# DeepFM + CIN on one core: four fields looked up by matrix products in place of three, their keys fetched by transfers, the weights' set-up rearranged, and the last tile's rows awaited alone

## What is computed

```python
emb = embed_table[f_ix, x_idx]                        # 2048 x 26 x 16
lin1 = w1_table[f_ix, x_idx].sum(axis=1, keepdims=True) + w1_bias
s = emb.sum(axis=1)
fm = 0.5 * ((s * s).sum(-1) - (emb * emb).sum(axis=(1, 2)))[:, None]
h = relu(emb.reshape(n, F * D) @ mlp_w1 + mlp_b1)     # 416 -> 400
h = relu(h @ mlp_w2 + mlp_b2)                         # 400 -> 400
deepfm = lin1 + fm + h @ mlp_w3 + mlp_b3
x0 = emb.transpose(0, 2, 1); last = x0; feats = []
for W in (cin_w0, cin_w1, cin_w2):                    # 128 x 26 x 26, then 128 x 128 x 26 twice
    last = einsum('ndl,ndf,klf->ndk', last, x0, W)
    feats.append(last)
return deepfm + concatenate(feats, -1).sum(1) @ lin_w + lin_b
```

## Time and profile before

| | before |
|---|---|
| median of 3 runs | 530.3 us (530.12 to 530.62) |
| the profiled execution: time | 530.45 us |
| the profiled execution: span of the core | 528.6 us |
| mean granted TensorE clock | 0.968 |
| TensorE matmuls busy | 468.6 us, 89% |
| VectorE busy | 376.7 us, 71% |
| ScalarE busy | 361.6 us, 68% |
| GpSimd busy | 364.6 us, 69% |

### The profile page before, as it was taken

One profiled execution on the slowest core, in us unless ns is written; L12 is line 12 of the kernel. 1 busy time (PEld: TensorE's weight loads), 2 busy tenths in 40 slices (PEclk: granted clock), 3 DMA queues, 4 the chain that ended last, 5 costly groups with the idle time before them and its releaser, 6 DMA issues. The chain is left out here.

```text
span 528.6 us, 6627 instructions
## 1 busy us (share of the span) xinstructions
PE 468.6 (89%) x2230; PEld 384.6 (73%) x2230; DVE 376.7 (71%) x610; ACT 361.6 (68%) x707; POOL 364.6 (69%) x382
## 2 busy tenths in 40 slices
PE   0798499899898989899999989898989899998895
PEld 0795367588787878687877878787868687787684
DVE  6811265869687786868686968778686868695766
ACT  1002459878686877777676868786777767677883
POOL 5777787877777777777777777777777777774000
PEclk9999559899999999999999999999999999999998
DMA  8973652122222222222222222222222222221000
GB/s 179 237 133 26 82 132 8 5 8 7 9 7 9 7 8 7 9 7 9 7 8 7 8 8 8 8 8 8 8 8 8 8 8 7 8 8 6 0 2 1
DMA packets 21550, 13.63 MB, mean 26 GB/s; under 512 B 12792, under 2 KB 20493, under 8 KB 21261
## 3 DMA queue, kind: packets, MB, share of 16 engines
q0 software_dynamic: 12064, 3.31, 18.4%
q1 hardware_dynamic: 5863, 7.92, 6.4%
q10 hardware_dynamic: 3590, 1.99, 2.0%
HBM read 13.00 MB, written 0.19 MB: 25 GB/s over the span
## 5 line engine op out<-in xcount | busy, mean ns | idle before, releaser
L417 POOL DMA_INDIRECT emb<-rows,idx_raw x377 | 364.3, 966 | 117.4 <-issue 114.6
L660 DVE TENSOR_TENSOR z_lo<-ps_s,z_hi 128x512 fp32r<-128x512 f32 (+1 forms) x192 | 130.7, 687 | 66.5 <-ACT ps_s L483 65.1
L476 ACT ACTIVATE z_hi<-ps_s 128x512 fp32r<-128x512 f32 (+1 forms) x192 | 114.4, 596 | 78.7 <-PE ps_s L908 77.8
L483 ACT ACTIVATE ps_s<-ps_s 128x512 f32<-128x512 f32 (+1 forms) x192 | 113.9, 593 | 0.7
L922 PE MATMUL ps_q<-z_lo,zw_hi 128*127 128x512 f32 (+1 forms) x192 | 86.0, 448 | 15.9 <-DVE z_lo L660 14.4
L923 PE MATMUL ps_q<-z_hi,zw_lo 128*127 128x512 f32 (+1 forms) x192 | 76.4, 398 | 0.0
L924 PE MATMUL ps_q<-z_hi,zw_hi 128*127 128x512 f32 (+1 forms) x192 | 76.3, 397 | 0.0
L908 PE MATMUL ps_s<-xt,pick 128*128 128x512 f32 (+1 forms) x192 | 74.3, 402 | 0.4 <-DVE xt L652 0.4
L922 PEld LDWEIGHTS ps_q<-z_lo,zw_hi 128*127 128x127 f32 (+1 forms) x192 | 36.4, 190 | 32.4 <-DVE z_lo L660 19.7
L994 PE MATMUL ps_y<-look_hi,one_hot 128*128 128x442 f32 (+1 forms) x156 | 56.3, 361 | 2.3 <-DVE one_hot L754 2.3
L995 PE MATMUL ps_y<-look_lo,one_hot 128*128 128x442 f32 (+1 forms) x156 | 54.8, 353 | 0.0
(11 more groups left out here) (165 smaller groups left out, 757.2 us busy)
## 6 DMA issues: line engine op xcount, KB each, us to landing
emb<-rows,idx_raw POOLq DMA_INDIRECT x377, 3.0
w_space<-rows SPq DMA_DIRECT2D x2, 728.9 KB
m_raw<-mlp_w SPq DMA_DIRECT2D x2, 650.0 KB
w<-cin_w SPq DMA_DIRECT2D x1, 832.0 KB, 6.7
w<-cin_w ACTq DMA_DIRECT2D x1, 832.0 KB, 13.2
w_space<-cin_w SPq DMA_DIRECT2D x1, 832.0 KB, 15.0
w_space<-cin_w ACTq DMA_DIRECT2D x1, 832.0 KB, 18.4
m_raw<-rows SPq DMA_DIRECT2D x1, 728.9 KB
```

Of the source, the lines that this page charges most:

```text
L417: pool.indirect_dma_start(emb[t % EMB][:, f, :], None, rows, bass.IndirectOffsetOnAxis(row_ix[:, t, f:f + 1], 0)).then_inc(gathered[t], 16)
L476: act.activation(z_hi[0:k, c, :], ps[0:k, :], ACT.Square)
L483: act.activation(ps[0:k, :], ps[0:k, :], ACT.Square).then_inc(hi_ready, 1)
L660: dve.tensor_tensor(z_lo[0:k, u % NC, :], ps_s[s_no(t, u) % RING][0:k, :], z_hi[0:k, u % NC, :].bitcast(F32), ALU.subtract).then_inc(lo_re ...
```

## The change

- LOOKS is 4: from tile 3 on, 22 fields are gathered and 4 looked up. The split of the tables, KEYS, ROWS and PICKED get new steps; the one-hot is now made in the step that KEYS names; the last `pick_row` stands in `start_tile` ahead of the first `z_low`.
- Keys: TensorE's `keys` is gone. Once, all keys are transposed, copied and stored to DRAM; then SyncE fetches each tile's four rows of keys to all partitions (`key_row`), two buffers.
- Set-up: `cin_w2` comes in two halves of its rows k, and `cin_w1` is issued when the first half has landed; TensorE does 52 half-size products. The blocks of pairs are stored by six transfers (`leave`) and brought back by six (`move`). `m2_raw` shares space with `w2` and is loaded and split during tile 0.
- The second MLP layer's rows are cut 128, 128, 128 and 16; the last chunk holds high and low parts stacked, 10 products in place of 12.
- `x_high` makes only the fp32r copy; the plain copy `x_full` follows the first `square` and is waited for by the second and third `picked`.
- The last tile: its first 18 gathers have their own semaphore; ScalarE copies by position in three parts after the last `square` of tile 14, and TensorE does `hidden2` and `sum_products` of tile 14 ahead of `x_half`; VectorE's `start_last` does all of tile 14 first.

The diff, cut to its core:

```diff
-LOOKS = 3
+LOOKS = 4
+EARLY = 18
-        LOOK_SPLIT = {4: 0, 6: 1, 8: 2}
-        KEYS = {1: 0, 5: 1, 9: 2}
-        ROWS = {3: 0, 7: 1, 11: 2}
-        PICKED = {5: 0, 9: 1}
+        LOOK_SPLIT = {3: 0, 5: 1, 7: 2, 9: 3}
+        KEYS = {4: 0, 7: 1, 9: 2, 11: 3}
+        ROWS = {3: 0, 6: 1, 8: 2, 11: 3}
+        PICKED = {6: 0, 9: 1, 11: 2}
...
+        def move(eng, n):
+            name, g, c0, col, ab, n_b, n_c, n_d = BLOCKS[n]
+            n_a = GROUPS[g]
+            eng.wait_ge(y_stored[n], 16)
+            eng.dma_start(moved[0:n_a * n_c, g, col:col + n_b * n_d].rearrange("p (b d) -> p b d", d=n_d),
+                          bass.AP(y_dram[n].tensor, y_dram[n].offset,
+                                  [[n_d, n_a * n_c], [n_a * n_c * n_d, n_b], [1, n_d]])).then_inc(moved_in[g], 16)
...
-            sp.dma_start(w2[0:HALF_P], cin_w2[0:HALF_P]).then_inc(w2_in, 16)
+            for h in range(2):
+                ls = slice(HALF_P * h, HALF_P * (h + 1))
+                sp.dma_start(w2[0:HALF_P, ls], cin_w2[0:HALF_P, ls]).then_inc(w2_in[h], 16)
+            sp.wait_ge(w2_in[0], 16 * 2)
...
+            for t in range(FIRST_LOOK, T):
+                if t >= FIRST_LOOK + 2:
+                    sp.wait_ge(one_hot_ready, look_no(t - 2, LOOKS))
+                sp.dma_start(key_row[t % 2], key_dram[LOOKS * t:LOOKS * (t + 1), :].partition_broadcast(P)
+                             ).then_inc(keys_in[t % 2], 16)
...
             def x_high(t, h):
-                act.activation(x32[t % 2][LO * h:LO * h + XR], ps, ACT.Copy)
+            def x_full(t, h):
+                act.wait_ge(lo_ready, x_no(t, h) + 1)
+                act.activation(x32[t % 2][LO * h:LO * h + XR], ...
...
+            x_full(0, 0)
+            x_full(0, 1)
             act.wait_ge(m1_in, 16 * 3)
             act.activation(m1_hi[0:XK], m1_raw[0:XK], ACT.Copy).then_inc(m1_hi_ready, 1)
...
                     if looks(t + LEAD):
                         if u in PICKED:
                             pick_row(t + LEAD, PICKED[u])
-                        if u - 2 in KEYS:
-                            keys_to_one_hot(t + LEAD, KEYS[u - 2])
+                        if u in KEYS:
+                            keys_to_one_hot(t + LEAD, KEYS[u])
...
                 add_third(t - 1)
+                if looks(t - 1 + LEAD):
+                    pick_row(t - 1 + LEAD, LOOKS - 1)
                 z_low(t, 0)
                 add_product(t - 1, NQ - 1)
                 z_low(t, 1)
                 fold(t - 1)
                 hidden2(t - 1)
-                if looks(t - 1 + LEAD):
-                    pick_row(t - 1 + LEAD, 2)
                 z_low(t, 2)
...
             def look_rows(t, i):
+                if n:
+                    pe.wait_ge(looked, n)
                 pe.wait_ge(one_hot_ready, n + 1)
...
+                    if after == T - 1:
+                        hidden2(t)
+                        sum_products(t)
+                        x_half(after, 0)
+                        x_half(after, 1)
```

More of the change, by code:

```diff
@@ L515, in start_tile @@
                 x_high(t, 1)
-                for u in range(NC):
-                    square(t, u)
+                square(t, 0)
+                x_full(t, 0)
+                x_full(t, 1)
+                square(t, 1)
+                square(t, 2)
             act.wait_ge(b_done, 1)
@@ L728, in tile, with start_last @@
                             pick_row(t + LEAD, PICKED[u])
-                        if u - 2 in KEYS:
-                            keys_to_one_hot(t + LEAD, KEYS[u - 2])
+                        if u in KEYS:
+                            keys_to_one_hot(t + LEAD, KEYS[u])
+            def start_last():
+                t = T - 1
+                times_left(t - 1, NQ - 1)
+                times_third(t - 1)
+                add_third(t - 1)
+                add_product(t - 1, NQ - 1)
+                fold(t - 1)
+                hidden2(t - 1)
+                x_low(t, 0)
+                x_low(t, 1)
+                for u in range(NC):
+                    z_low(t, u)
             def start_tile(t):
```

276 lines of the change are left out of this document (172 added, 104 removed).

## The result

The changed kernel takes **559.4 us** (median of 4 runs, 558.0 to 560.3) against 530.2 (530.0 to 530.6) for the one before, measured beside it: 1.055 times as long, interval 1.052 to 1.057. My prediction was 543.3, with a range of 508 to 551. The sign and the places were right, the size wasn't: +12.9 us were forecast, +29 came. The profiled execution of the change took 558.02 us, with a span of 556.2; the one before had 528.6.

The account below looks back on a forecast made before the run. Bound: the 77.1 us set-up, then TensorE's order of work with small waits. Set-up -11.6, tile 0 +3.1, 13 look-up tiles +20.2, end +1.2: +12.9 on 530.45, so 543.3 us; range 508 to 551, the forecast's own 532 to 551.

Parts of the forecast that it names:

- Set-up, forecast -11.6: Start to first `main`: 65.5 in place of 77.12, -11.6 us (-14.1 to -5.4).
- the runs of the transfers would put the sum at 57.7: Set-up: if the 4,059 runs were the cost, the last sum comes at 57.7, ending 6 us later.
- 14.0 from that sum to the first `main`: Set-up: ScalarE's and VectorE's operations in a row from the last sum of blocks to the first `main`, 14.0 us.
- Tile 0, forecast +3.1: Tile 0: ScalarE gets a fourth table and the second layer's split, +3.1 us (0 to +3.5).
- (a): Look-up tile, last look-up's products to `main` of step 2: 8.55 us, -1.1.
- (b): Look-up tile, step 2 to step 4: 6.4 us now, called unchanged, yet -0.1.
- (c): Look-up tile, step 4 to step 8: second look-up's one-hot waited for 1.05 us, a `keys` saved, +0.85.
- (d): Look-up tile, step 8 to last look-up's products: third look-up's work, waits of 0.36 and 0.7 us, +1.95.
- 2.7 longer than overlapped, 1.5 to 4: Tile 14's join to tile 15, run one thing after another: 2.7 us longer than overlapped, 1.5 to 4.
- the waits don't materialise: Rival 1, look-up tiles: ScalarE or VectorE runs further ahead, tile 27.5 us, total 509 (505 to 529); chance 0.28.
- the gathers become the bound: Rival 2: quick set-up and tiles of 27 bring tile 15 near 468, total 501 us; chance 0.05.
- the clock falls within tiles: Rival 3: TensorE falls to 1.2 GHz within tiles; at 0.95 in 13 tiles 20 us more, above 555; chance 0.04.

Follow-up runs that it names:

- the filling products: Unused products of the identity with the tables ahead of the sums; six, with spaced look-ups (four in three tiles, else three), old join, later `x_full`: 523.3 us.
- the move: `x_full` put behind `m1_hi` in the set-up of the changed kernel, run only with other edits; with look-ups three steps apart and the old join: 537.9 us.

## Why the prediction was wrong in size

The forecast missed 14.8 of the 27.7 us: 6.3 in the tiles with look-ups, 3.8 at the end, 3.4 in the set-up and 1.3 in tile 0. The waits for one-hots, on which it rested, came as forecast; what failed are terms that were left out or put too small around them.

*Set-up, forecast -11.6, measured -8.2.* Two steps. The last sum was to come at 51.5 and came at 52.74; that is inside the bounds I gave. TensorE started at 10.57, where I had 10, and its half-size products did cost half each (the 52 take 11.54 us, the 26 before 11.91). A move took longer to issue than the 0.37 I priced: SyncE's three took 3.05 us, ScalarE's three 1.97. That the runs of the transfers would put the sum at 57.7 didn't come true. The step that failed is "14.0 from that sum to the first `main`"; it took 16.17. I had added up ScalarE's and VectorE's operations (sums, `x_low`, the copy, `m1_hi`, `m1_lo`, clearing, low parts). They do run in that order, and `m1_lo` starts 5.8 us behind the last sum where it started 2.3 behind it before; but TensorE's row products, which my sum left out, are longer: 9.7 us from 52.32, then `picked`, zlin and za to 67.8. In the kernel before, the first group had run ahead of the last two sums, while their transfers were still out; only 6.6 us of products lay behind 63.62. Now the three sums start within 1.2 us of each other, and all products lie behind them, 3.2 us more (52.32 to 55.48), which is about what the distance grew by (13.38 to 16.17). So the moves' gain reached the first `main` only in part. That TensorE and its clock set this chain is shown by the filling products (12.64 us from the sum with six, where it was 16.17); that `x_full` and `m1_hi` don't, by the 16.15 with and without the move. With the clock up, TensorE waits 2.38 us at the end instead of 1.15. That isn't the chain I had summed either: with six filling products `m1_lo` has ended by 57.1, while ScalarE waits 3.92 us for the row products and then does copies and squares until 63; `zw_lo` stands behind these.

The clock by the rows: it was 0.50 from 52 to 62 us behind a stretch with 1.12 us of work in 6 (46 to 52), and 1.00 when that stretch was filled. The Trainium skill (TensorE: Matmul & The Clock Gate, Part 1) says that the gate opens by how busy the array has been lately; the trace agrees. The same part of the Trainium skill puts the cost of the ramp under 1% of a typical kernel; the 5.2 us counted above are 1.0% of 530 here, and enough to matter in a tuned one.

*Tile 0, forecast +3.1, measured +4.4.* ScalarE is busy 24.65 us of 29.68, as against 21.96 of 25.32; the work I named is there. The end of the tile adds a wait of TensorE of 2.2 us for `x_low`, behind the fourth table's and the second layer's low parts, VectorE's share of the same work, which I hadn't counted. And the clock had no term: TensorE's 86 instructions are busy for 23.48 us at a granted clock of 0.79, where they were for 22.11 at 0.85, which is 1.4 of the 4.4 us.

*A tile with look-ups, forecast 30.1, measured 30.53.* The four stretches in tile 2, forecast and measured: (a) 8.55, 8.68; (b) 6.3, 6.40; (c) 8.14, 8.25; (d) 7.15, 7.22. The waits in (c) and (d) were forecast at 1.05, 0.36 and 0.7. The profile lists 0.94 and 0.59 as idle time; counted as the forecast counts, from start to start less the usual 0.23, the three are 1.11, 0.27 and 0.76, together 2.14 for 2.11. So the mechanism, the places and the waits stand. What was mis-sized is the rest, by 0.07 to 0.13 in each of the four stretches. Two pieces have a name. In (a) `x_full`, costed at 0, is waited for by 0.41 us, and VectorE's second `z_low` then waits 0.34 for ScalarE. In (b) I had written -0.1 without a reason, and it takes 6.40 as before. The rest, some 0.2, has none that a run shows. 30.53 - 30.12 = 0.41 over 13 tiles is 5.3 of the 6.3 missing; the other 0.9 is that the tiles of the kernel before average 370.54 / 13 = 28.50, where I had taken tile 2's 28.57 for all.

*The end, forecast +1.2, measured +5.0.* The step that failed is "2.7 longer than overlapped, 1.5 to 4". I had listed the chain rightly but for `x_full`, and taken most of it for hidden. Three waits of 2.22, 1.05 and 2.25 are open, and the clock falls in them, so that a product of `main` takes 0.63 us, where it takes 0.40, until the clock is back at some 531.7. The `x_full` copies in the third of them take 1.20 us. Undoing the join gave back 6.4 us, over the top of the bounds.

*The rivals.* That the waits don't materialise was refuted directly (1.5 us a tile). That the gathers become the bound wasn't so with four look-ups: the last gather starts at 473.5 and its tile's copies at 517. But it is just what happens once the fourth look-up is gone, so the 9 us of spare time in the earlier trace rows were the whole reserve for any gain in the tiles or the set-up that leaves the number of gathers as it is. That the clock falls within tiles was wrong for those with look-ups (1.00). It fell in tile 0, at the join and in the set-up, and none of these terms had a price for it.

*Where the change's gain is.* Without the fourth look-up its other parts make the kernel faster by 0.5%, and without the new join too by 1.2%. Those parts save 0.85 us in a tile; which of them does wasn't tested one by one. The fourth look-up costs 1.7 us a tile as best placed here, in a kernel whose TensorE is the bound, and saves 1.27 us of a GpSimd that isn't; as it was placed it cost 2.8.

## What to carry to other kernels

When work is moved from an engine with spare time to the one that bounds, price the move on the bound first, and find out where the spare time of the other ends: here the best kernel has four look-ups in a few tiles and three in the rest. For work that goes round through two engines with one buffer (products, take-out, one-hot, products), look at what each link stands behind in its engine's order, and at the distance to the link before; mending the first alone moved the wait to the closest pair. And before a chain that hangs on one late transfer, look at what the waiting engine could have done with the parts that came first, and at the clock it will have when it starts.
